# Macaron block on one core: weight splits eight periods later, pair 1's maxima spread over attention's first period, norm steps one per period

## The reference

```python
x = x + 0.5 * ffn(layernorm(x))          # mixture of experts: 2 shared, 8 routed, top 2, with a capacity
x = x + attention(layernorm(x))          # 16 heads of 64, rope and a Fourier term on q and k, softmax, w_out
x = x + 0.5 * ffn(layernorm(x))          # the same weights again
# attention, per batch:
q, k, v = split(x @ w_qkv.T)             # 1024 columns each
q = q * cos + rotate_half(q) * sin + fenc   # k likewise
out = softmax(q @ k.T * scale) @ v       # per head, then @ w_out.T + b_out
```

## Time and profile before

| | us |
|---|---|
| median of 3 runs | 1322.57 (1318.83 to 1326.94) |
| the profiled execution | 1320.95 |
| its span, first to last instruction | 1318.2 |
| TensorE busy | 1265.1 |
| VectorE busy | 864.8 |
| ScalarE busy | 613.6 |
| GpSimd busy | 883.4 |

### The profile page before, as it was taken

The page is one execution under the profiler, slowest core; times in us unless marked ns, Lnnn a source line. Parts: engine busy times, 40 slices in busy tenths (PEclk is TensorE's granted clock), DMA queues, the critical chain, the costliest instruction groups (busy, mean ns, idle before and its releaser), DMA issues.

```text
span 1318.2 us, 21651 instructions
## 1 busy us (share of the span) xinstructions
PE 1265.1 (96%) x7858; PEld 783.6 (59%) x7858; DVE 864.8 (66%) x1378; ACT 613.6 (47%) x917; POOL 883.4 (67%) x652
## 2 busy tenths in 40 slices
PE   5979999799999999999999999999999999899998
PEld 3656666455565565656565656566655655566665
DVE  6636687658887666666666666666687874565632
ACT  3434532445545445455545554545545454433422
POOL 0424347677797888888888889788878872444353
PEclk9989999999999999999999999999999999999999
DMA  5441241123223232323232322323223221432240
GB/s 163 129 177 42 88 140 22 32 42 63 60 58 66 50 74 50 73 51 73 50 63 61 61 62 58 66 50 73 50 57 66 52 56 18 145 137 74 72 153 16
DMA packets 118680, 95.39 MB, mean 72 GB/s; under 512 B 75760, under 2 KB 85008, under 8 KB 118320
## 3 DMA queue, kind: packets, MB, share of 16 engines
q1 hardware_dynamic: 118576, 94.01, 28.9%
HBM read 57.53 MB, written 2.88 MB: 46 GB/s over the span
## 4 chain that ended last, share of the span: by engine, by line
PE 83%; DVE 6%; issue 4%; DMA 3%; POOL 2%; ACT 1%; SPq 0%; DVEq 0%; ACTq 0%; POOLq 0%
PE banks L1124 15%; PE banks L451 15%; PE banks L1107 12%; PE banks L464 9%; PE banks L1139 6%; PE banks L1058 6%; PE banks L978 6%; PE banks L1112 4%; PE banks L1148 4%; PE banks L986 3%; PE banks L1090 1%; DMA work<-in_w_v 1%; DVE side L1284 1%; DMA den_c<-den_d 1%; PE banks L413 1%
## 5 line engine op out<-in xcount | busy, mean ns | idle before, releaser
L990 DVE TENSOR_REDUCE neg_max<-banks 128x2 f32<-128x1024 f32 x256 | 313.4, 1224 | 101.8 <-PE banks L978 95.5
L1217 ACT ACTIVATE work<-banks 128x1024 f32<-128x1024 f32 x256 | 251.0, 1026 | 173.1 <-PE banks L1112 173.0
L1372 POOL TENSOR_TENSOR turn<-turn,side_turned 128x512 f32<-128x512 f32 x128 | 160.9, 1279 | 129.9 <-DMA side_turned<-side 129.9
L1124 PE MATMUL banks<-work 128*64 128x512 f32 x1024 | 233.8, 598 | 0.0
L1366 POOL TENSOR_TENSOR turn<-turn,fenc 128x512 f32<-128x512 f32 x128 | 162.0, 1288 | 13.0 <-DVE side L1284 12.8
L1377 POOL TENSOR_TENSOR qk_l<-turn,qk_h 128x512 fp32r<-128x512 f32 x128 | 162.2, 1289 | 7.3 <-ACT qk_h L967 7.3
L1382 POOL TENSOR_TENSOR work<-work 128x1024 f32<-128x1024 f32 x64 | 152.9, 2389 | 9.5 <-PE banks L1124 9.5
L1124 PEld LDWEIGHTS banks<-work 128*64 128x64 f32 x1024 | 67.8, 136 | 133.0 <-issue 110.1
L799 POOL TENSOR_TENSOR o_raw<-o_raw,work 128x512 f32<-128x512 f32 x52 | 67.0, 1290 | 98.5 <-DVE o_raw L718 98.4
L978 PE MATMUL banks<-qk_h 64*128 64x512 f32 x512 | 115.9, 449 | 6.6 <-DVE neg_max L990 5.7
L799 POOL TENSOR_TENSOR work<-work 128x512 f32<-128x512 f32 x44 | 56.5, 1293 | 93.8 <-DVE work L718 50.4
(11 more groups left out here) (173 smaller groups left out, 2399.3 us busy)
## 6 DMA issues: line engine op xcount, KB each, us to landing
work<-share SPq DMA_DIRECT2D x32, 1024.0 KB, 9.3
side_turned<-side SPq DMA_DIRECT2D x256, 128.0 KB, 3.0
rec_all<-rec_d SPq DMA_DIRECT2D x128, 128.0 KB, 3.1
x_tok<-in_x SPq DMA_DIRECT2D x8, 256.0 KB, 6.4
out<-x_tok SPq DMA_DIRECT2D x8, 256.0 KB, 9.2
work<-in_w_gate_up SPq DMA_DIRECT2D x1, 1280.0 KB, 7.4
work<-in_w_qk SPq DMA_DIRECT2D x1, 1024.0 KB, 9.6
den_d<-den_rows SPq DMA_DIRECT2D x64, 4.0 KB
```

The lines of the kernel that those rows point to most:

```text
L990: return nc.vector.tensor_reduce(neg_max[:, g % 2, qt::DH], of, AX.X, ALU.max, negate=True)
L1124: ins = nc.tensor.matmul(O[OWN[h], :], v_all[:, kt, n * DH:(n + 1) * DH], pt[:, g % 2, kt, h * T:(h + 1) * T], start=(kt == 0), stop=(kt = ...
L1217: nc.scalar.activation(pt[:, g % 2, kt, :], S[kt].rearrange("p h q -> p (h q)"), ACT.Exp, scale=QSCALE).then_inc(s["probs"], 1)
L1372: nc.gpsimd.tensor_tensor(turn[:, g % 2, part], turn[:, g % 2, part], side_turned[:, part], ALU.add).then_inc(done, 1)
```

## The change

1. QK_FROM goes from -48 to -40: the eight q/k splits on ScalarE and VectorE are in unit periods 30, 34, ..., 58. Those of pair 7 now come after the v splits. The waits for counts are unchanged.
2. Attention's first period on TensorE has an order of its own, `first_period`. Pair 1's maxima 0 and 1 no longer stand ahead of it. VectorE's order is unchanged.
3. The statistics of both late norms are split in two periods each (5 and 6; 23 and 25), and each later stage has a period of its own: 7 to 23 without 12 and 20, and 26 to 56 where p % 8 is 0, 1, 2 or 6. Since the second norm now starts while the first one's results are still to be read, the first one's `rs` is copied to `rs_end`. Two waits at the start of the second norm are gone.

```diff
-JOIN_NORM_AT = {53: (0,), 54: (1, 2), 55: (3, 4, 5), 56: (6, 7), 57: (8, 9), 58: (10, 11), 59: (12, 13), 60: (14, 15)}
+JOIN_STATS_AT = {23: range(0, 4), 25: range(4, 8)}
+JOIN_NORM_AT = {p: (n,) for n, p in enumerate([p for p in range(26, 60) if p % 8 in (0, 1, 2, 6)], 1) if n < LN_STAGES}
...
-                            if last:
-                                dve.wait_ge(att["xn_ready"], B - 1)
...
-                if ahead in JOIN_NORM_AT:
+                if ahead in JOIN_STATS_AT:
+                    if 0 in JOIN_STATS_AT[ahead]:
+                        routed.mark(nc.vector.memset(count[:], 0.0))
+                        routed.mark(nc.vector.memset(count_b[:], 0.0))
+                    statistics(JOIN_STATS_AT[ahead], 0)
+                elif ahead in JOIN_NORM_AT:
                     norm_first(JOIN_NORM_AT[ahead])
...
-            QK_FROM, V_FROM = -48, -14
+            QK_FROM, V_FROM = -40, -14
...
-            END_AT = {4: (0,), 5: (1, 2), 6: (3, 4), 7: (5, 6), 8: (7, 8), 9: (9, 10), 10: (11, 12), 12: (13, 14, 15)}
+            END_STATS_AT = {5: range(0, 4), 6: range(4, 8)}
+            END_AT = {p: (n,) for n, p in enumerate([p for p in range(7, 28) if p % PAIRS != 4], 1) if n < LN_STAGES}
...
+                def first_period():
+                    maxima(1, 0)
+                    scores(0, 0)
+                    scores(0, 1)
+                    maxima(1, 1)
+                    project_both(3, 0)
+                    maxima(1, 2)
+                    values(0)
+                    maxima(1, 3)
+                    turn_maxima(1, 0)
+                    maxima(2, 0)
+                    scores(0, 2)
+                    scores(0, 3)
+                    maxima(2, 1)
...
                     pe.wait_ge(ffn1["x_done"], B)
-                    maxima(1, 0)
-                    maxima(1, 1)
                     for p in PERIODS:
...
-                    rs_of, shift_of = (rs_c, shift_end) if late >= 0 else (rs_all, shift_all)
+                    rs_of, shift_of = (rs_end, shift_end) if late >= 0 else (rs_all, shift_all)
...
                     for n in END_AT.get(p, ()):
-                        if n == 0:
-                            for t in range(CT):
-                                statistics(dve, t, stats_c, B - CB)
-                        else:
-                            small_step(n, CT, mean_c, rs_c, shift_end)
+                        if n == LN_STAGES - 1:
+                            steps.wait()
+                            steps.mark(nc.vector.tensor_copy(rs_end[:], rs_c[:]))
+                        small_step(n, CT, mean_c, rs_c, shift_end)
```

More of the change, by code:

```diff
@@ L127, in macaron @@
         shift_end = sb("shift_end", [P, CT])
+        rs_end = sb("rs_end", [P, CT])
         work = sb("work", [P, 3 * 4096])
@@ L639, in dve, with statistics @@
                 per_tile = lambda ap: ap.unsqueeze(1).broadcast_to([P, CT, E])
+                def statistics(tiles, c):
+                    for j in tiles:
+                        steps.mark(nc.vector.bn_stats(stats_c[:, j, :], x_tok[:, CB * c + j // TT, j % TT, :]))
                 def norm(n, c):
@@ L643, in norm @@
                         at_least(dve, s["xn_ready"], CB * c - 1)
-                        for j in range(CT):
-                            steps.mark(nc.vector.bn_stats(stats_c[:, j, :], x_tok[:, CB * c + j // TT, j % TT, :]))
+                        statistics(range(CT), c)
                     elif n < LN_STAGES - 1:
@@ L1150, in project_out @@
                     ins.then_inc(s["y_ps"], 1)
+                def first_period():
[12 more added lines that the diff above has]
+                    maxima(2, 1)
                 def period(p):
                     new, ahead, nxt, last = p + 3, p + 2, p + 1, p - 1
+                    if p == 0:
+                        first_period()
+                        return
                     if exists(nxt):
@@ L1310, in end_norm @@
                 def end_norm(p):
+                    for t in END_STATS_AT.get(p, ()):
+                        statistics(dve, t, stats_c, B - CB)
                     for n in END_AT.get(p, ()):
-                        if n == 0:
-                            for t in range(CT):
-                                statistics(dve, t, stats_c, B - CB)
-                        else:
-                            small_step(n, CT, mean_c, rs_c, shift_end)
+                        if n == LN_STAGES - 1:
+                            steps.wait()
+                            steps.mark(nc.vector.tensor_copy(rs_end[:], rs_c[:]))
+                        small_step(n, CT, mean_c, rs_c, shift_end)
                 def period(p):
@@ L1326, in period @@
                     end_norm(p)
-                    if p in JOIN_NORM_AT:
+                    if p in JOIN_STATS_AT or p in JOIN_NORM_AT:
                         ffn2["vector"](dve, p)
```

## The result

The changed kernel takes 1305.10 us, the median of four runs (1304.11 to 1306.16), against 1321.47 us for the kernel before (1318.83 to 1326.94, four runs). The ratio is 0.9871, its 95% interval 0.9837 to 0.9905. Forecast were 17.8 us less and 1304.8. The profiled execution took 1305.81 us with a span of 1303.3, which is 14.9 less than the span before; the account by stages explains these 14.9.

A forecast was written before the change was run, and what follows sets the result against it. TensorE, busy 96% of the span, was taken as the bound, so only its waits could be gained. -9.17 + 1.2 - 2.0 - 8.85 + 1.0 = -17.8 us from 1322.57 gave 1304.8; range 1298 to 1313.

The forecast's parts named there:

- pair 1's maxima: Start of attention: the new order brings the third maxima of period 1 earlier; 2.0 us gained, bounds 0.8 to 2.2.
- the stall: First FFN: TensorE stands behind ScalarE's first weight split, waiting for weights; later splits gain 9.17 us, bounds 0 and 9.6.
- the norm steps: Attention periods with late-norm statistics and steps: spreading them saves 8.85 us less 1.0 left over.
- the inverted order: First norm of attention's input: pair 7's split behind v's delays VectorE; 1.2 us lost, bounds 0.8 and 3.5.
- The absent split of period 26: First FFN: no split in period 26 might give 0.4 us more, making the upper bound 9.6.
- The fourth rival: First norm: the splits' inverted order costs 3.5 us in place of 1.2, giving 1307.1; chance 0.12.
- the term for the clock: Attention's start: a clock fall in the new order's thin stretch costs up to 1.2 us, leaving 0.8 in place of 2.0.
- the leftover: Norm-step periods after spreading: 1.0 us of cost remains, bounds 0 and 7.2.
- the threes: Norm-step periods with three operations: four in the new lists at 0.16 us each, 0.6 in sum.
- The first rival: Norm-step periods: operations in threes keep their price, 7.2 us in place of 1.0, giving 1311.0; chance 0.12.
- the second: Rival: all 30 periods with a norm step cost one GpSimd instruction, 1.29 us each, giving 1343.5; chance 0.04.
- The other rivals: First FFN: the stall comes back elsewhere, 1309.4, chance 0.07; or it stays because weights land later, 1314, chance 0.02.

The follow-up runs named there:

- filler: The changed kernel with 15 matmuls that nobody reads laid into the waits of attention's first period: 1304.16 us, ratio 0.9874 to the kernel before.
- old_filler: The changed kernel with the old order of attention's first period and 20 unread matmuls in its four waits for reductions: 1302.64 us.
- first_only: The kernel before with only the new order of attention's first period: 1319.64 us, ratio 0.9996.
- splits_only: The kernel before with QK_FROM = -40 alone: 1311.01 us, ratio 0.9921.
- all_three: The changed kernel with unread matmuls in attention's first period, V_FROM = 2 and the xn_odd operations spread over periods 57 to 60: 1298.35 us.

## Why the prediction was right, and where it was not

The time was right to 0.3 us, and that closeness is luck. Forecast were 17.8 us less than a median of 1322.57; with its fourth run the kernel before has 1321.47, so the gain in medians is 16.4. The gain between the two profiles, 14.9, misses the 17.8 by 2.9. Against the forecast's sum, pair 1's maxima gave 3.6 less, the way from the transposes to attention 0.4 less and the time from period 61 on 0.9 less; the stall gave 0.4 more, the norm steps 0.8, the inverted order 0.1 and periods 13 to 52 0.6. The lower end of the range was added wrongly (9.6, 2.2 and 8.85 less 0.8 are 19.85, not 20.5); nothing hangs on it.

**The stall: right.** Forecast 9.17, at most 9.6; measured 9.56. The absent split of period 26 would account for the 0.4, as the bound said; no run shows it apart.

**The inverted order: right in size and place.** Forecast 1.2; measured 1.12 at the transposes. The first low part ends 0.84 us later against TensorE's stream than before (forecast 0.8), and pair 7's low part adds 0.4. Only the sign by which I meant to see it was wrong: TensorE's wait for the norm is 1.85 us and not 2.9, since it lost part of the 1.12 before, in the late products of units 57 and 58 (one wait of 0.32 for them is new). The fourth rival (3.5) is out.

**Pair 1's maxima: the step that failed.** Forecast 2.0 gained, between 0.8 and 2.2; the profile has 0.97 lost up to the first apply_v and 0.59 in the periods behind it, and alone the part gives 0.9996. The layout of the new order was right: with the clock at 1.00, in `filler`, the third maxima of period 1 come 14.19 us after the first matmul (forecast 14.1). What failed is the term for the clock. The 2.15 compare a new start at full clock with an old start that had lost 1.5 us to the lower one (18.79 against the 17.28 of `old_filler`); the order itself hides 0.57. The sum put the new start's own loss at nothing and the bound at 1.2 at most. It was 2.6 to 3.1 in all seven profiles, since the clock stays low for 10 to 14 us. The forecast had the place right: in all seven the clock falls in the new thin stretch, 7 to 11 us behind the first matmul. What it missed is how long it stays low. In after that lasts through 6 us of nearly gapless work, the next wait (1.32 us, before 251.45) and the start of apply_v; in before the clock was back at 1.00 by 252, ahead of the wait before 253.40. Why it stays low for longer in the new order is not shown. The rule named in the forecast (the Trainium skill, "TensorE: Matmul & The Clock Gate", Part 1: the lower clock is the default, activity releases it) agrees in its direction with the fillers, which kept the clock at 1.00; by it I gave 0.8 at least, and that was still too much.

**The norm steps: the mechanism right, the leftover too large.** Forecast 8.85 less 1.0; the profile has 8.67 gained with 0.2 left over. In after the threes cost nothing. They cost where they start late or stand beside a new batch: period 55 of `first_only` 1.1 us, and period 12, which the forecast's count of threes left out, 1.1 in before, 0.9 in `splits_only` and in `first_only`. The new lists use no period with a new batch. The first rival (threes keep their price) is out; so is the second, since none of the 30 periods has an excess in after. (In other profiles with the spread steps a single period is 0.3 to 0.9 us long now and then, also periods with one operation, such as 22 in `all_three`.) In the medians this part is 6.6 us (4.4 to 9.0), as the gain itself varies with the old kernel's luck. A 128 x 8 operation took up to 2.40 us beside GpSimd and 0.16 without. The rule of the Trainium skill ("GPSIMD Engine Reference", section 1: VectorE operations with two SBUF inputs or in a 2-port mode contend with GpSimd for its SBUF interfaces) agrees.

**What the forecast did not see.** Period 61 holds the same kind of crowd, in four operations instead of six. Against the 12.11 us without it, it cost 1.7 us in the one profile read and 2.0 to 5.0 in later ones; the largest prices are those with a fall of the clock behind it.

**The other rivals.** The stall did not come back elsewhere, nor stay.

## What to carry to other kernels

Where a bounded engine waits for a queue in which small operations stand ahead of the needed one, count the operations in one period and the neighbour's instructions that they can meet: six tiny ones cost 0.7 to 5.9 us here, three mostly nothing and at worst 1.1. Spreading work also takes out scatter, so compare the scatter of runs and not only medians. A wait of TensorE has two prices, its own length and what the clock does behind it: when an order is laid out to hide waits, look at whether what remains of the gaps is spread thin, and price the lower clock for the whole stretch behind it. Before two profiles are compared, compare the granted clock behind each wait.

## What the runs showed that I had not expected

Two periods with the same six operations, the same late spread and the same waits of TensorE cost 3.1 to 3.6 us with the clock at 1.00 and 5.8 to 5.9 with a fall to 0.50; which of the two an execution gets is open. At the start of attention the clock stayed at 0.50 even in a stretch of 4.00 us that was busy from end to end (252 to 256 in after). And 15 to 20 matmuls that compute nothing made the start 1.4 to 3 us shorter.
